# A four-sequence language block: products with Wm, rank rows and the place matrix put ahead of and into the selected attention

## The chip, the cores and the metric

The kernel runs on one core of one Trainium2 chip. The metric is the device time of one execution in microseconds (us), taken as the median of several runs.

## The reference, cut to what matters

The whole is two transformer-like layers over 4 sequences of 1024 tokens with 192 features. The change touches the second half of the first layer (`_L0_ffn_ref`), which routes tokens: 154 of 1024 tokens with the lowest scores get attention, all others a cheap mix.

```python
normed = _ln(hidden_states, g1, b1)
scores = sigmoid(einsum('bld,d->bl', normed, Wr) + br)
_, idx = top_k(-scores, k)            # k = 154
attn_mask = zeros((b, l), bool).at[arange(b)[:, None], idx].set(True)
...                                   # attention of 12 heads over all keys
attn_out = ctx @ Wo + bo
w = scores / (sum(scores, axis=1, keepdims=True) + 1e-06)
pooled = einsum('bl,bld->bd', w, normed)
mix_out = (normed + scores[..., None] * pooled[:, None, :]) @ Wm + bm
merged = where(attn_mask[..., None], attn_out, mix_out)
h = hidden_states + merged
n2 = _ln(h, g2, b2)
ffn = gelu(n2 @ W1 + bf1) @ W2 + bf2
return h + ffn
```

`hidden_states` is itself a layer norm of the stream h, so the kernel needs that norm again for the residual.

## The kernel before, in words

Sequences go in two pairs (loop `p`), and within a pair each sequence has a slot, 0 (`a`) and 1 (`z`). Each engine has its own program, written by hand, and they meet through counting semaphores; nothing is reordered. A sequence is 8 token tiles of 128 tokens (`T = 8`). `XT` holds the normed tokens feature-major (two halves of 96 features and a row of ones for the bias), `X` the normed tokens token-major, `U` the layer's branch to add to `HS`, the stream.

PSUM has eight banks of 512 float32. The four of `ST` are a ring (`ring4`, two for each slot as `o.R2`). Each slot also has two banks `o.D2`: `PV` or `MT`, and `S`.

The order around the change, by TensorE:

- `logits` and `scores_row`: the scores; they are turned into a row (`srow`) and give the pooled sum.
- VectorE `rank_tokens`: compares the score row with each tile's scores; this yields the rank of each token, `notsel` (rank is 154 or more), and `PSEL`, the matrix which gathers the selected tokens. `pool_tokens` follows.
- `pick`: gathers the selected tokens with `PSEL` (L621). ScalarE writes `NTS`.
- `queries0`: queries of the selected tokens in the ring banks (L554), then `values` of all tokens in `o.D2` (L569). ScalarE and VectorE cut the queries into three bfloat16 parts, and SP stores and reloads them in another layout.
- `mix_in` (VectorE, L1440): adds score times pooled vector to `XT`, once `values` has read it.
- `selected`: 6 groups of 4 heads. VectorE reduces ten banks of scores to maxima a group (L1471), alternately in the two `S` banks; TensorE makes the scores (L649, L652), the exponents' arguments (L672) and the sums over values (L685). TensorE's loop `g` issues the maxima of group g+1; those of group 0 come ahead of the loops. Keys of group g+2 are reloaded by DMA once the exponents of group g are through.
- `context` turns the result and, behind it, the ranks (L749). `attended` multiplies with Wo (L757), giving `ATS`.
- `pick_rows` (VectorE): the place matrix `PT` from the turned ranks in PSUM, 8 instructions for the two slots (L1485), and `U` as the norm of `HS` (L1488).
- `mix` and `merge`: for each token tile, the product with Wm (L770) and the placing product `PT` by `ATS` (L772) in the two halves of one bank; VectorE adds the first times `notsel` (L1495), then the second (L1496). Statistics, norm and `turn_norm` follow (L1359, L1369, L536), then the feed-forward (`up`, `back`).

Each call of a float32 matmul appears as two products in the trace, so a token tile's product with Wm is four.

## Time and profile before

| | |
|---|---|
| median of 3 runs | 2040.24 us (2032.58 to 2041.11) |
| the profiled execution | 2034.34 us, of which the span is 2032.3 us |
| TensorE busy | 1658.6 us, 82% of the span |
| VectorE busy | 1377.1 us, 68% |
| ScalarE busy | 955.2 us, 47% |
| GpSimd busy | 126.8 us, 6% |

Busy shares are means over stages with different limits. The granted clock is that of TensorE: 1.00 is 2.4 GHz and 0.50 is 1.2 GHz. Durations of neighbours on one engine overlap by up to 0.2 us, so the time between two starts is the rate.

### The profile page before, as it was taken

What the parts mean: (1) busy time and instruction counts of PE and PEld (TensorE: products, weight loads), DVE (VectorE), ACT (ScalarE), POOL (GpSimd) and SP (SyncE); (2) the same over time, 40 slices, a digit from 0 to 9 for tenths busy, and PEclk for the clock granted to TensorE, in tenths of its full rate; (3) what the DMA queues carried; (4) which work ended last, traced back from release to release, by engine and by line L of the source; (5) the groups of instructions that cost most, each with busy time, mean ns of one, the idle gap of its engine ahead of it and who ended that gap; (6) DMA issues with size and microseconds to landing.
All of it is one profiled execution on the core that took longest, in us unless ns stands there. A gap on an engine that the chain in (4) does not pass through costs nothing.

```text
span 2032.3 us, 26452 instructions
## 1 busy us (share of the span) xinstructions
PE 1658.6 (82%) x9798; PEld 940.1 (46%) x9798; DVE 1377.1 (68%) x3124; ACT 955.2 (47%) x1347; POOL 126.8 (6%) x165
## 2 busy tenths in 40 slices
PE   1676888998999999964456968889899999999444
PEld 1355657564343333363243655766533333336423
DVE  4758565026898989677768576531489989894876
ACT  0421450214777777732532315221357777775153
POOL 5010000000000000005020000000000000000200
PEclk9966895999999999986568778779989999999756
DMA  6003210007001000001010312000431010000001
GB/s 145 1 1 109 76 33 0 0 1 217 24 25 32 24 29 28 1 1 31 0 32 0 109 45 63 1 0 0 125 101 32 24 32 25 24 16 1 0 0 32
DMA packets 53894, 73.39 MB, mean 36 GB/s; under 512 B 18712, under 2 KB 27205, under 8 KB 53767
## 3 DMA queue, kind: packets, MB, share of 16 engines
q1 hardware_dynamic: 52150, 68.54, 11.6%
q0 software_dynamic: 1616, 3.16, 0.7%
q8 instruction: 79, 1.29, 0.3%
q14 instruction: 49, 0.39, 0.1%
HBM read 38.51 MB, written 33.17 MB: 35 GB/s over the span
## 4 chain that ended last, share of the span: by engine, by line
PE 65%; DVE 26%; ACT 3%; issue 3%; DMA 1%; SPq 1%; POOL 0%; DVEq 0%; ACTq 0%
PE PV L888 9%; PE ST L872 8%; PE S L838 6%; PE ST L784 4%; PE ST L554 4%; PE MT L838 3%; PE PV L897 2%; DVE Er L1557 2%; DVE st L1359 2%; PE S L795 2%; DVE nmp L1471 2%; DVE R L1577 2%; DVE amax L1578 2%; PE ST L581 1%; PE S L833 1%
## 5 line engine op out<-in xcount | busy, mean ns | idle before, releaser
L1194 ACT ACTIVATE Er<-ST 128x1024 f32<-128x1024 f32 x384 | 377.0, 1021 | 105.9 <-PE ST L872 105.7
L1533 DVE TENSOR_REDUCE nmp<-S 128x1 f32<-128x512 f32 x514 | 337.2, 682 | 30.8 <-PE S L838 30.8
L872 PE MATMUL ST<-QS,KS 100*128 100x512 bf16 x768 | 218.1, 386 | 0.3
L888 PE MATMUL PV<-Er,V 128*17 128x512 f32 x1536 | 211.8, 601 | 0.0
L838 PE MATMUL S<-KS,QS 96*128 96x512 bf16 x514 | 183.5, 392 | 0.8
L1533 DVE TENSOR_REDUCE nmp<-MT 128x1 f32<-128x512 f32 x254 | 173.2, 682 | 13.5 <-PE MT L838 13.5
L838 PEld LDWEIGHTS S<-KS,QS 96*128 96x128 bf16 x514 | 48.3, 98 | 154.8 <-DVE nmp L1533 118.1
L448 POOL TENSOR_SCALAR tp<-mv 128x8 f32<-128x8 f32 x20 | 5.2, 258 | 1735.7 <-DVE mv L1363 1735.7
L872 PEld LDWEIGHTS ST<-QS,KS 100*128 100x128 bf16 x768 | 72.1, 99 | 64.3 <-ACT Er L1194 5.7
L838 PE MATMUL MT<-KS,QS 96*128 96x512 bf16 x254 | 99.5, 392 | 0.8 <-DVE nmp L1533 0.8
L1471 DVE TENSOR_REDUCE nmp<-S 128x1 f32<-128x512 f32 x120 | 76.5, 684 | 30.7 <-PE S L649 28.6
L784 PE MATMUL ST<-XT,wf 96*128 96x512 f32 x192 | 84.0, 594 | 0.0
L996 PE MATMUL S<-identb,Er 128*128 128x128 bf16 x192 | 24.9, 304 | 72.2 <-DVE Er L1593 72.2
L1161 ACT ACTIVATE Er<-ST 128x480 f32<-128x480 f32 x144 | 64.6, 540 | 31.7 <-PE ST L672 31.5
L1388 DVE TENSOR_TENSOR acc_out<-ST,R 96x512 f32<-96x512 f32 x48 | 32.8, 684 | 67.7 <-ACT R L1115 56.6
L1105 ACT ACTIVATE XT<-PV,cols 96x512 f32<-96x512 f32 x8 | 6.2, 774 | 150.9 <-PE PV L536 150.9
L1212 ACT ACTIVATE R<-ST 128x512 f32<-128x512 f32 x48 | 28.7, 597 | 93.5 <-PE ST L784 93.5
L1501 DVE TENSOR_TENSOR HS<-PV,HS 128x384 f32<-128x384 f32 x8 | 4.5, 557 | 92.5 <-PE PV L796 82.7
L1294 ACT ACTIVATE Er<-S 128x768 bf16<-128x768 bf16 x32 | 25.5, 810 | 80.5 <-PE S L996 80.5
L1196 ACT ACTIVATE Er<-ST 100x1024 f32<-100x1024 f32 x48 | 49.1, 1023 | 28.3 <-PE ST L876 28.3
L888 PEld LDWEIGHTS PV<-Er,V 128*17 128x17 f32 x1536 | 32.4, 96 | 62.2 <-issue 60.5
L1177 ACT ACTIVATE acc_out<-PV 128x512 f32<-128x512 f32 x96 | 57.4, 597 | 7.0 <-PE PV L888 7.0
(392 smaller groups left out, 3285.1 us busy)
## 6 DMA issues: line engine op xcount, KB each, us to landing
KS<-scr_k SPq DMA_DIRECT2D x72, 192.0 KB, 2.6
scr_k<-R SPq DMA_DIRECT2D x16, 576.0 KB, 4.0
QS<-scr_q SPq DMA_DIRECT2D x48, 192.0 KB, 2.8
scr_k<-R SPq DMA_DIRECT2D x16, 384.0 KB, 4.6
QS<-scr_k SPq DMA_DIRECT2D x24, 192.0 KB, 2.6
scr_q<-R SPq DMA_DIRECT2D x8, 576.0 KB, 4.5
scr_k<-R SPq DMA_DIRECT2D x16, 192.0 KB, 5.2
scr_q<-R SPq DMA_DIRECT2D x8, 384.0 KB, 4.9
```

Of the source, the lines that this page charges most:

```text
L554: ins = nc.tensor.matmul(o.R2[i % 2][0:CH, 0:width], w[0:r, c, off + m * CH:off + (m + 1) * CH], src[0:r, c, j * width:(j + 1) * width], s ...
L784: ins = nc.tensor.matmul(o.R2[i % 2], wf1[0:r, c, f * P:(f + 1) * P], o.XT[0:r, c, half * HALF:(half + 1) * HALF], start=c == 0, stop=c == 1)
L795: nc.tensor.matmul(d, o.hid[:, f, t % HT * P:(t % HT + 1) * P], wf2[:, f, :], start=f == 0, stop=False)
L838: ins = nc.tensor.matmul(bank, QS[0:KP, k, (u // 2) * P:(u // 2 + 1) * P], KS[0:KP, k, (u % 2) * HALF:(u % 2 + 1) * HALF], start=True, sto ...
L872: ins = nc.tensor.matmul(ST[i % 2][:, (kt % 2) * HALF:(kt % 2 + 1) * HALF], KS[0:KP + 4, k, kt * P:(kt + 1) * P], QS[0:KP + 4, k, half * H ...
L888: ins = nc.tensor.matmul(PV[row:row + VC, :], slots[h // H].V[:, kt, h % H, :], E[:, step % RING, (kt % 2) * HALF:(kt % 2 + 1) * HALF], st ...
L1161: A_(E0[:, h % RING0, i * 6 * QP:i * 6 * QP + w], ring4[n % 4][:, 0:w], ACT.Exp, scale=float(DH) ** -0.5).then_inc(s["ex0"], 1)
L1177: A_(acc_out[:, part, :], PV[:, :], ACT.Copy).then_inc(s["accout"], 1)
L1194: A_(E[:, g, :], ST[i % 2][:, :], ACT.Exp).then_inc(s["exps"], 1)
L1196: A_(E[0:MS, g, :], ST[i % 2][0:MS, :], ACT.Exp).then_inc(s["exps"], 1)
L1471: v.tensor_reduce(nmp[:, x // 2, x % 2:x % 2 + 1], S[n % 2][:, :], AX.X, ALU.max).then_inc(s["reduced0"], 1)
L1533: v.tensor_reduce(nmp[:, u // 2, u % 2:u % 2 + 1], bank, AX.X, ALU.max).then_inc(s["reduced"], 1)
```

## The change

Seven edits go together.

1. `values` for both slots runs ahead of `pick`, in the ring banks; `queries0` of a slot follows that slot's `pick`.
2. `mix_in` runs ahead of the cut of the queries, and computes `back`, the ratio of the two norms' scales.
3. The products with Wm (`premix`) come after the queries of slot 1. ScalarE evicts them times `notsel` into `U` (`precopy`).
4. The ranks are turned into the ring banks (`turn_rank`), and ScalarE copies them to SBUF (`rank_row`).
5. In `selected`, VectorE puts one instruction (`aside`) behind every second reduction of groups 0 to 3: 16 additions of `X` times `back` into `U`, and 4 rows of the place matrix, now one instruction of 1024 columns from SBUF each.
6. `context` no longer turns the ranks, and `pick_rows` is gone.
7. `mix` has the placing products alone, two tiles a bank, and `merge` adds a bank's two tiles in one instruction.

```diff
@@ -185,6 +185,7 @@
             o.spl = R[0:CH, 0:3 * L].bitcast(BF16).rearrange("p (a c n) -> p a c n", a=3, c=2)
             o.srow = R[:, 3 * L:4 * L]
             o.PT = R[:, 0:2 * L].rearrange("p (q n) -> p q n", q=2)
+            o.rrow = R[:, 2 * L:3 * L]
             o.hid = R[:, 0:FC * HALF].rearrange("p (f n) -> p f n", f=FC)
             o.kc = R[0:CH, 0:3 * HALF].bitcast(BF16).rearrange("p (a n) -> p a n", a=3)
             o.qc = R[0:CH, 3 * HALF:6 * HALF].bitcast(BF16).rearrange("p (a n) -> p a n", a=3)
@@ -217,6 +218,7 @@
             o.cnt = sb("cnt" + nx, [P, 3, T])
             o.rank = sb("rank" + nx, [P, T])
             o.notsel = sb("notsel" + nx, [P, T])
+            o.back = sb("back" + nx, [P, T])
             o.pool3 = sb("pool3" + nx, [CH, 8])
             o.amax = sb("amax" + nx, [P, T])
             o.qsc = sb("qsc" + nx, [P, T])
@@ -560,13 +562,16 @@
 
             def values(p, o, use, w, off):
 
+                banks = (o.R2, o.D2)[use]
+                if use == 0:
+                    pe.wait_ge(s["srow_copied"], at(p, o, 1, 1))
                 for i in range(4):
                     if i >= 2:
                         pe.wait_ge(o.s["vcopied"], p * 8 + 4 * use + i - 1)
                     for t in (2 * i, 2 * i + 1):
                         for c in range(2):
                             r = CH + c
-                            ins = nc.tensor.matmul(o.D2[i % 2][:, (t % 2) * D:(t % 2 + 1) * D], o.XT[0:r, c, t * P:(t + 1) * P],
+                            ins = nc.tensor.matmul(banks[i % 2][:, (t % 2) * D:(t % 2 + 1) * D], o.XT[0:r, c, t * P:(t + 1) * P],
                                                    w[0:r, c, off:off + D], start=c == 0, stop=c == 1)
                     ins.then_inc(o.s["vproj"], 1)
 
@@ -624,10 +629,27 @@
 
             def queries0(p, o):
                 pe.wait_ge(s["nts"], at(p, o, 2, 2))
-                pe.wait_ge(s["srow_copied"], at(p, o, 1, 1))
+                pe.wait_ge(o.s["vcopied"], p * 8 + 4)
                 project(p, o, 4, wq, 0, o.NTS, 2 * QP, 1)
-                values(p, o, 0, wv, 0)
-
+
+            def premix(p, o):
+
+                pe.wait_ge(s["mixin"], at(p, o, 2, 2))
+                for i in range(4):
+                    if i >= 2:
+                        pe.wait_ge(s["precopied"], at(p, o, 4, i - 1))
+                    for t in (2 * i, 2 * i + 1):
+                        for c in range(2):
+                            r = CH + c
+                            ins = nc.tensor.matmul(o.D2[i % 2][:, (t % 2) * D:(t % 2 + 1) * D], o.XT[0:r, c, t * P:(t + 1) * P], wm[0:r, c, :], start=c == 0, stop=c == 1)
+                    ins.then_inc(s["premixed"], 1)
+
+            def turn_rank(p, o):
+
+                pe.wait_ge(o.s["resid"], p * 14 + 6)
+                for t in range(T):
+                    ins = nc.tensor.transpose(o.ST[:, t * P:(t + 1) * P], o.rank[:, t:t + 1].to_broadcast([P, P]), ident[:])
+                ins.then_inc(s["rank_turned"], 1)
 
             def selected(p):
                 base = p * ROWS
@@ -705,10 +727,11 @@
                             turn_sums(a, SUMS0_AT[x])
 
                 for q in slots:
-                    pe.wait_ge(q.s["vcopied"], p * 8 + 4)
-                    pe.wait_ge(q.s["resid"], p * 14 + 6)
+                    pe.wait_ge(s["precopied"], at(p, q, 4, 4))
                 maxima0(0, 0, MAXIMA0)
                 maxrow0(0)
+                for q in slots:
+                    pe.wait_ge(s["rank_copied"], at(p, q, 1, 1))
                 pe.wait_ge(s["qones"], p + 1)
                 for g in range(GROUPS):
                     n = 3 * GROUP * g
@@ -745,9 +768,6 @@
                     for q in range(2):
                         ins = nc.tensor.transpose(o.R2[0][0:CH, (2 * c + q) * QP:(2 * c + q + 1) * QP], o.CX[:, q, c * CH:(c + 1) * CH], ident[0:QP, 0:QP])
                 ins.then_inc(s["ctxt"], 1)
-                for t in range(T):
-                    ins = nc.tensor.transpose(o.D2[t // HT][:, t % HT * P:(t % HT + 1) * P], o.rank[:, t:t + 1].to_broadcast([P, P]), ident[:])
-                ins.then_inc(s["rank_turned"], 1)
 
             def attended(p, o):
                 pe.wait_ge(s["ctxtc"], at(p, o, 1, 1))
@@ -758,18 +778,15 @@
                 ins.then_inc(s["att"], 1)
 
             def mix(p, o):
-                pe.wait_ge(s["mixin"], at(p, o, 2, 2))
+
                 pe.wait_ge(s["pt"], at(p, o, 1, 1))
                 pe.wait_ge(s["atts"], at(p, o, 1, 1))
-                for t in range(T):
-                    if t >= 2:
-                        pe.wait_ge(s["merged"], at(p, o, 8, t - 1))
-                    d = o.D2[t % 2]
-                    for c in range(2):
-                        r = CH + c
-                        nc.tensor.matmul(d[:, 0:D], o.XT[0:r, c, t * P:(t + 1) * P], wm[0:r, c, :], start=c == 0, stop=c == 1)
-                    for q in range(2):
-                        ins = nc.tensor.matmul(d[:, D:2 * D], o.PT[0:QC, q, t * P:(t + 1) * P], o.ATS[0:QC, q, :], start=q == 0, stop=q == 1)
+                for i in range(4):
+                    if i >= 2:
+                        pe.wait_ge(s["merged"], at(p, o, 4, i - 1))
+                    for t in (2 * i, 2 * i + 1):
+                        for q in range(2):
+                            ins = nc.tensor.matmul(o.D2[i % 2][:, (t % 2) * D:(t % 2 + 1) * D], o.PT[0:QC, q, t * P:(t + 1) * P], o.ATS[0:QC, q, :], start=q == 0, stop=q == 1)
                     ins.then_inc(s["mixed"], 1)
 
             def up(p, o, half):
@@ -1019,9 +1036,14 @@
                 for o in slots:
                     scores_row(p, o)
                 for o in slots:
+                    values(p, o, 0, wv, 0)
+                for o in slots:
                     pick(p, o)
-                for o in slots:
                     queries0(p, o)
+                for o in slots:
+                    premix(p, o)
+                for o in slots:
+                    turn_rank(p, o)
                 selected(p)
                 for o in slots:
                     context(p, o)
@@ -1117,10 +1139,26 @@
                         mid(i - 1)
                 mid(group + len(pieces) - 1)
 
+            def precopy(p, o):
+
+                act.wait_ge(s["picks"], at(p, o, 2, 2))
+                for i in range(4):
+                    act.wait_ge(s["premixed"], at(p, o, 4, i + 1))
+                    for t in (2 * i, 2 * i + 1):
+                        ins = A_(o.U[:, t, :], o.D2[i % 2][:, (t % 2) * D:(t % 2 + 1) * D], ACT.Copy, scale=o.notsel[:, t:t + 1])
+                    ins.then_inc(s["precopied"], 1)
+
+            def rank_row(p, o):
+                for n in ("kw0", "kw1"):
+                    act.wait_ge(o.s[n], p * 96 + 48)
+                act.wait_ge(s["rank_turned"], at(p, o, 1, 1))
+                A_(o.rrow[0:QC, :], o.ST[0:QC, :], ACT.Copy).then_inc(s["rank_copied"], 1)
+
             def vcopy(p, o, use):
+                banks = (o.R2, o.D2)[use]
                 for i in range(4):
                     act.wait_ge(o.s["vproj"], p * 8 + 4 * use + i + 1)
-                    A_(o.V[:, 2 * i:2 * i + 2, :, 0:DH], o.D2[i % 2][:, 0:2 * D].rearrange("p (t h d) -> p t h d", t=2, h=H), ACT.Copy).then_inc(o.s["vcopied"], 1)
+                    A_(o.V[:, 2 * i:2 * i + 2, :, 0:DH], banks[i % 2][:, 0:2 * D].rearrange("p (t h d) -> p t h d", t=2, h=H), ACT.Copy).then_inc(o.s["vcopied"], 1)
 
             def inproj(p, o, c):
                 for i in range(4):
@@ -1238,12 +1276,17 @@
                     act.wait_ge(s["srow_turned"], at(p, o, 1, 1))
                     A_(o.srow, o.ST[:, :], ACT.Copy).then_inc(s["srow_copied"], 1)
                 for o in slots:
+                    vcopy(p, o, 0)
+                for o in slots:
                     act.wait_ge(s["gathersel"], at(p, o, 1, 1))
                     for c in range(2):
                         A_(o.NTS[0:CH, c, :], o.S[0:CH, c * 2 * QP:(c + 1) * 2 * QP], ACT.Identity, scale=cols[:, c, 2:3], bias=cols[:, c, 3:4]).then_inc(s["nts"], 1)
                 for o in slots:
                     cut(p, o, 4, pieces_q0(o), 2 * QP)
-                    vcopy(p, o, 0)
+                for o in slots:
+                    precopy(p, o)
+                for o in slots:
+                    rank_row(p, o)
                 selected(p)
                 for o in slots:
                     act.wait_ge(s["ctxt"], at(p, o, 1, 1))
@@ -1436,6 +1479,8 @@
 
             def mix_in(p, o):
                 ve.wait_ge(o.s["vproj"], p * 8 + 4)
+                link(v.reciprocal(o.back[:], o.rnn[:]))
+                v.tensor_tensor(o.back[:], o.back[:], o.rn[:], ALU.mult)
                 for c in range(2):
                     v.scalar_tensor_tensor(out=o.XT[0:CH, c, :], in0=o.srow[0:CH, :], scalar=o.pool3[:, 5 + c:6 + c], in1=o.XT[0:CH, c, :],
                                            op0=ALU.mult, op1=ALU.add).then_inc(s["mixin"], 1)
@@ -1464,6 +1509,19 @@
                         ins = v.tensor_tensor(dst, o.sum0[:, 2 * n:2 * n + 2, 0:DH], o.rec0[:, 2 * n:2 * n + 2].unsqueeze(2).to_broadcast([QP, 2, DH]), ALU.mult)
                     ins.then_inc(s["ctxn"], 1)
 
+                def aside(o, n):
+
+                    if n < T:
+                        if n == 0:
+                            ve.wait_ge(s["precopied"], at(p, o, 4, 4))
+                        v.scalar_tensor_tensor(out=o.U[:, n, :], in0=o.X[:, n, :], scalar=o.back[:, n:n + 1], in1=o.U[:, n, :], op0=ALU.mult, op1=ALU.add)
+                        return
+                    if n == T:
+                        ve.wait_ge(s["rank_copied"], at(p, o, 1, 1))
+                    ins = v.tensor_scalar(o.PT[0:QC, n - T, :], o.rrow[0:QC, :], rowslot[0:QC, n - T:n - T + 1], None, ALU.is_equal)
+                    if n == T + 1:
+                        ins.then_inc(s["pt"], 1)
+
                 for g in range(GROUPS):
                     for x in range(MAXIMA0):
                         n = MAXIMA0 * g + x
@@ -1471,6 +1529,8 @@
                         v.tensor_reduce(nmp[:, x // 2, x % 2:x % 2 + 1], S[n % 2][:, :], AX.X, ALU.max).then_inc(s["reduced0"], 1)
                         if g == GROUPS - 1 and x in SUMS0_AT:
                             divide(a, SUMS0_AT[x])
+                        if x % 2 == 1 and g < 4:
+                            aside(slots[g // 2], g % 2 * 5 + x // 2)
                     ve.wait_ge(s["reduced0"], p * MAXIMA0 * GROUPS + MAXIMA0 * g + MAXIMA0 + 2)
                     if g >= 2:
                         ve.wait_ge(s["mturned"], base + g - 1)
@@ -1478,23 +1538,11 @@
                 for r in range(3):
                     divide(z, r)
 
-            def pick_rows(p, o):
-                ve.wait_ge(s["rank_turned"], at(p, o, 1, 1))
-                for q in range(2):
-                    for j in range(2):
-                        ins = v.tensor_scalar(o.PT[0:QC, q, j * HALF:(j + 1) * HALF], o.D2[j][0:QC, :], rowslot[0:QC, q:q + 1], None, ALU.is_equal)
-                ins.then_inc(s["pt"], 1)
-                for t in range(T):
-                    ins = v.tensor_scalar(o.U[:, t, :], o.HS[:, t, :], o.mv[:, t, 0:1], o.rn[:, t:t + 1], ALU.subtract, ALU.mult)
-                link(ins)
-
             def merge(p, o):
-                for t in range(T):
-                    ve.wait_ge(s["mixed"], at(p, o, 8, t + 1))
-                    d = o.D2[t % 2]
-                    link(v.scalar_tensor_tensor(out=o.U[:, t, :], in0=d[:, 0:D], scalar=o.notsel[:, t:t + 1], in1=o.U[:, t, :], op0=ALU.mult, op1=ALU.add))
-                    v.tensor_tensor(o.U[:, t, :], o.U[:, t, :], d[:, D:2 * D], ALU.add).then_inc(s["merged"], 1)
-                ve.wait_ge(s["merged"], at(p, o, 8, 8))
+                for i in range(4):
+                    ve.wait_ge(s["mixed"], at(p, o, 4, i + 1))
+                    v.tensor_tensor(o.U[:, 2 * i:2 * i + 2, :], o.D2[i % 2][:, 0:2 * D].rearrange("p (t d) -> p t d", t=2), o.U[:, 2 * i:2 * i + 2, :], ALU.add).then_inc(s["merged"], 1)
+                ve.wait_ge(s["merged"], at(p, o, 4, 4))
                 stats(p, o, o.U)
 
             def add(o, i, done):
@@ -1629,11 +1677,10 @@
                     rank_tokens(p, o)
                     pool_tokens(p, o)
                 for o in slots:
+                    mix_in(p, o)
+                for o in slots:
                     cut(p, o, 4, pieces_q0(o), 2 * QP)
-                    mix_in(p, o)
                 selected(p)
-                for o in slots:
-                    pick_rows(p, o)
                 for o in slots:
                     merge(p, o)
                 for o in slots:
```

## Rows read from the trace of the kernel before

**Rows 1.** The page: shares of the chain that ended last, by engine.

```profile
PE 65%; DVE 26%; ACT 3%; issue 3%; DMA 1%; SPq 1%; POOL 0%; DVEq 0%; ACTq 0%
```

**Rows 2.** Windows of the tail: each engine's busy time, granted clock, DMA share, GB/s.

```profile
293.40:349.50 56.10, 45.42 (x180) 44.16 (x180) 32.14 (x113) 1.84 (x4) 2.91 (x4) 0.63 0.00 1
...
1283.00:1339.00 56.00, 45.37 (x180) 44.12 (x180) 32.09 (x113) 1.84 (x4) 2.86 (x4) 0.63 0.00 1
...
308.40:349.50 41.10, 36.19 (x112) 35.68 (x112) 18.09 (x69) 0.00 (x0) 2.91 (x4) 0.50 0.00 1
```

**Rows 3.** Timeline of TensorE in the tail: start, duration, instruction, idle before it.

```profile
297.51 0.48 PE L746 MATMUL ST<-ident,small 80*96 80x80 f32 x4 [1.49 <-DVE small L1464]
...
298.71 2.78 PE L757 MATMUL ST<-wo,NTS 96*80 96x192 f32 x16
...
308.38 1.65 PE L770 MATMUL PV<-wm,XT 96*128 96x192 f32 x4 [4.29 <-DVE U L1496]
...
343.10 1.49 PE L772 MATMUL S<-ATS,R 77*128 77x192 f32 x4
349.51 1.09 PE L536 MATMUL PV<-ident,X 128*96 128x128 f32 x4 [4.92 <-DVE X L1369]
```

**Rows 4.** Timeline of VectorE in the tail.

```profile
296.96 0.49 DVE L1464 TENSOR_TENSOR small<-X 80x32 f32<-80x32 f32 x4
...
321.59 0.42 DVE L1495 SCALAR_TENSOR_TENSOR U<-PV,notsel,U 128x192 f32<-128x192 f32 x1 [1.75 <-PE PV L772]
...
345.47 2.18 DVE L1359 BATCH_NORM_STATS2 st<-U 128x6 f32<-128x192 f32 x8
```

**Rows 5.** Timeline of TensorE ahead of the selected attention.

```profile
175.80 2.70 PE L614 MATMUL MT<-sc,ones 128*96 128x1 f32 x16
...
201.62 6.51 PE L621 MATMUL S<-Er,X 128*96 128x160 f32 x32 [10.63 <-DVE Er L1424]
207.96 1.26 PE L554 MATMUL ST<-NTS,wq 96*96 96x160 f32 x8
209.06 1.47 PE L569 MATMUL PV<-wv,XT 96*128 96x192 f32 x8
```

**Rows 6.** Timeline of VectorE there: end of pooling, cut, first maxima.

```profile
202.30 0.47 DVE L1435 SCALAR_TENSOR_TENSOR pool<-cols,pool 96x1 f32<-96x1 f32 x2
209.41 0.55 DVE L1388 TENSOR_TENSOR acc_out<-ST,small 96x160 f32<-96x160 f32 x2 [6.64 <-ACT small L1115]
...
221.14 2.48 DVE L1440 SCALAR_TENSOR_TENSOR XT<-R,pool,XT 96x1024 f32<-96x1024 f32 x2 [2.99 <-PE S L569]
223.54 6.67 DVE L1471 TENSOR_REDUCE nmp<-S 128x1 f32<-128x512 f32 x10
```

**Rows 7.** Windows of the output projection, which begins at 105.57 after 11.4 us idle.

```profile
105.50:108.30 2.80, 2.73 (x9) 2.73 (x10) 2.76 (x3) 0.00 (x0) 0.00 (x0) 0.50 0.00 0
...
111.60:114.30 2.70, 2.70 (x16) 2.70 (x17) 0.97 (x2) 0.00 (x0) 0.00 (x0) 1.00 0.00 0
```

**Rows 8.** Timeline of ScalarE: one copy of the values.

```profile
219.83 0.49 ACT L1123 ACTIVATE V<-MT 128x384 f32<-128x384 f32 x1 [1.15 <-PE MT L569]
```

**Rows 9.** Timeline of VectorE elsewhere: two instructions like new ones.

```profile
89.93 0.75 DVE L1406 TENSOR_SCALAR R<-R,cols 96x1024 f32<-96x1024 f32 x1
...
382.95 0.56 DVE L1501 TENSOR_TENSOR HS<-PV,HS 128x384 f32<-128x384 f32 x1 [26.56 <-PE PV L796]
```

**Rows 10.** Windows of the loops, the transposes and the feed-forward.

```profile
231.00:243.70 12.70, 12.17 (x90) 7.16 (x88) 7.15 (x13) 6.68 (x15) 0.00 (x0) 0.52 0.21 62
243.70:253.70 10.00, 8.01 (x117) 5.06 (x118) 6.80 (x13) 7.07 (x17) 0.00 (x0) 1.00 0.27 80
...
349.50:356.90 7.40, 6.92 (x32) 5.14 (x33) 6.85 (x14) 5.17 (x7) 0.97 (x1) 0.58 0.00 0
356.90:440.00 83.10, 83.10 (x320) 53.23 (x318) 6.72 (x24) 16.59 (x27) 1.90 (x2) 1.00 0.00 0
```

**Rows 11.** Timeline of TensorE: the first products of a new group's keys.

```profile
253.72 0.59 PE L649 MATMUL S<-QS 96*128 96x512 bf16 x2 [1.29 <-DMA QS<-scr_k]
```

More of the change, by code:

```diff
@@ L248, in build @@
         w2 = slots[0].R[0:CH, 0:2 * F].rearrange("p (t f) -> p t f", t=2)
-        names = """qones loaded consts tokens outproj h1 logit expz score srow_turned srow_copied picks rank_turned pt gathersel nts
+        names = """qones loaded consts tokens outproj h1 logit expz score srow_turned srow_copied picks rank_turned rank_copied premixed precopied pt gathersel nts
             units0 reduced0 units reduced rowmax mturned mcopied acc0 ctxr accout st0 ex0 pv0 ctxn ctxt ctxtc att atts
@@ L1021, in _ @@
                 for o in slots:
+                    values(p, o, 0, wv, 0)
+                for o in slots:
                     pick(p, o)
+                    queries0(p, o)
                 for o in slots:
-                    queries0(p, o)
+                    premix(p, o)
+                for o in slots:
+                    turn_rank(p, o)
                 selected(p)
```

## The prediction

> **What bounds the kernel now.** I read the page first, and in it the chain that ended last: it is 65% TensorE and 26% VectorE [rows 1]. No engine bounds the whole, so the change has to be read in the stages it touches. There are two pairs of sequences, and every engine works through a pair in the same order, so each stage counts twice; the windows have the tail stage of pair 1 at 56.1 us and 0.63 of the clock, and pair 2's at 56.0 and 0.63 [rows 2]. All other numbers below are of pair 1.
>
> The tail stage runs from the last turned sums of the selected attention (293.4) to the first transpose of the third norm (349.5). TensorE's timeline [rows 3] and VectorE's [rows 4] show what sets it. VectorE ends the last division at 297.4. TensorE still turns the ranks, then does `attended` (298.71 to 301.32), fills slot 0's two banks and waits 4.29 us until VectorE has made the place rows and U. From 308.38 to 344.4 it then runs 28 groups of four products back to back, and VectorE waits 1.75 us for each later token tile [rows 4]. In this stretch the granted clock is 0.50, the 1.2 GHz level [rows 2]: four products take 1.28 us (36.0/28), against 0.65 in the values' projection of the same width (1.47 for eight, of which 0.16 overlaps the next) [rows 3, 5]. So 16 of the 32 groups (the Wm half) and all the preparation on VectorE sit on the path. After them come statistics, X and the transposes: 345.47 to 349.51, 4.0 us [rows 3, 4].
>
> Ahead of the selected attention the chain is the ranking on VectorE, pick of slot 1 (201.62 to 208.1), slot 0's queries and values, slot 1's queries and values, and last the mixing of XT, which lets the first maximum start at 223.54 [rows 5, 6]. Before that pick TensorE is idle for 10.63 us (from 191.0), and the pooling ends at 178.5 [rows 5]; slot 0's pick lies between, as long as slot 1's.
>
> **The change, part by part.**
>
> *Values ahead of the picks, in the ring banks.* The values are 8 groups of 1.3 us. They begin at 178.5, after the pooling; the wait for the copied score row costs nothing, as that copy ran during the pooling. The clock is low there. The output projection, of the same width, also starts low, after 11.4 us idle: its first products are at 0.50, and from 6 us on, with waits between, 16 take 2.70 us at 1.00 [rows 7], so I take it that the clock rises after some 4 us. Taking that: 10.5 + 2 = 12.5 us, to 191. Slot 0's pick follows, then idle until slot 1's ranks at 201.6. Nothing is late. If the clock never rose, values would take 21 us (to 199.3), slot 0's pick 6.6 more, and slot 1's pick would start at 206 to 208 instead of 201.6: up to 6.4 us lost. If the shorter idle time kept the clock high in slot 1's pick, its 6.5 us could shrink to some 4.3: 2.2 won. I take zero, the pick as it was, since 4 us of idle are left in front of it and after as long an idle (the 4.29 us before 308.38) TensorE came back low [rows 3].
>
> *Mixing of XT before the query cut.* VectorE is free from 202.8 to 209.4 [rows 6]. Four mixing instructions of 1.24 and two small ones per slot make 5.8 us, to 208.6. It fits ahead of the cut at 209.4, which is set by ScalarE. Were it not to fit, every us over goes to the queries' reload.
>
> *Queries of slot 1, products with Wm, ranks turned.* After pick (208.1) ScalarE copies 0.9, queries take 1.1 [rows 5]: 210.2. Products with Wm: 8 groups x 1.31 = 10.5: 220.7. Their eviction by ScalarE, 16 copies of 192 columns, is bounded by half of the 384-column one's 0.49 and by the whole [rows 8], 0.5 to 1.0 a group, under TensorE's 1.31: hidden; without that cover it would be 8 us at most. Turning the ranks is two times eight columns of 128, by width 128/192 of 1.31, 0.9: 222.5. That also covers the new wait of the first maxima for the last of these copies. The first maximum follows 0.4 later, 222.9, where it was 223.54 as VectorE was still mixing XT: 0.6 won. The rank rows' copies (two of 1024 columns, some 1 us each from 0.49 for 384) wait also for the keys' stores, long issued; behind them is the maxima row's copy, needed only when the maxima of group 0 are reduced, so they are hidden. SP's queue gets slot 1's query store some 6 us sooner, and no DMA is added.
>
> *Twenty insertions on VectorE in the maxima of groups 0 to 3.* Sixteen additions into U have 192 columns; the nearest row is 0.42 from PSUM [rows 4], of which neighbours overlap some 0.08: 0.34 each. Four place rows of 1024 in SBUF: 0.75 [rows 9]. Group 0 runs alone, VectorE without a gap (223.54, ten in 6.67 [rows 6]), so 5 x 0.34 = 1.7 us go on the path. Group 1 is reduced while TensorE runs its first loop at the low clock, 12.7 us for VectorE's 7.15 [rows 10]: hidden. Groups 2 and 3 lie in loops of 10 us with 6.8 us of VectorE work [rows 10]. There the chain is: last exponent products of the loop, reload of the keys, next products at 253.72, 1.29 us late [rows 11]. Two insertions ahead of the second half move its last reductions by some 0.7 (two of 0.34), so 0.7 each loop. The two place rows of group 3 stand behind the reduction that TensorE waits for and (1.5) fall into the reload's wait, which itself moves by the 0.7. Sum: 1.7 + 0.7 + 0.7 = 3.1 lost. Bounds: 0 if all is hidden, 16 x 0.42 + 4 x 0.75 = 9.7 if nothing is.
>
> *The tail.* Removed: 16 rank transposes behind the context, eight place rows from PSUM and the sixteen of U, 64 products with Wm, and one of two VectorE steps a tile. Now: division ends 297.4, context 0.4, `attended` 2.6: 300.5. The first placing group is 0.65, its addition of 384 columns 0.56 [rows 9]. Two banks alternate at about 0.75 a group: slot 0's fourth addition ends at 304.0. Statistics 2.9: 306.9. Slot 1's first two groups wait ready; two additions 1.1 to 308.0; its other two groups start at 307.6 after 3 us of idle, taken at the low clock (1.28 each), last addition ended 310.9. Then 4.0 as before: 314.9 against 349.51, so 34.6 won. All placing at the high clock: 36; all at the low one: 31.6.
>
> Here a page speaks. The Trainium skill, TensorE: Matmul & The Clock Gate, What's actually happening, says that the clock is low by default and that activity releases it. The trace does not bear that out here, with 0.50 held over 36 us of busy products [rows 2, 3]. By the rule the placing would soon be fast and the tail's gain nearer 36 than 34.6.
>
> *Sum.* Per pair 34.6 + 0.6 - 3.1 = 32.1, for two 64.2. The profiled execution took 2034.34 us (span 2032.3): 1970.1. The median of the runs shown is 5.9 higher, which would give 1976. I say 1971.
>
> **Rivals.**
>
> *The loops fall to the low clock.* The first loop is at 0.52 with 12.7 us, the others at 1.00 with 10 [rows 10]. Insertions thin TensorE's work; if they keep it low for four more loops, 2.7 x 4 = 10.8 a pair. For it: the first loop stays low although busy. Against: loops 1 and 2 keep their 8.0 us of TensorE work and grow by only 0.7. Time: 2034.3 - 2 x 21.3 = 1992.
>
> *Values at the low clock.* The products of one column ahead of them are no dense work. Against: the output projection, which rose by itself [rows 7]. 6.4 a pair: 1983.
>
> *The low clock has a time of its own.* It held from 308 to 356 whatever ran. If it holds some 45 us after the short placing too, 30 to 35 us of the first feed-forward products run at half rate, 17 a pair lost: 2034.3 - 2 x 15 = 2004. Against: in the row of the transposes alone the clock rises (0.58 over the 7.4 us, 0.50 before, 1.00 after) [rows 2, 10]. The Trainium skill, same page, Part 4: PE-mode transpose, says that transposes do not engage the high clock, which would leave the feed-forward to begin low; by it a few us a pair are added, and the row just named speaks against it.
>
> *Slower than before.* The same low clock held through the whole feed-forward (83.1 us, all at 1.00 [rows 10]): each us of its work costs one more. It decides from 32 us of such work on (64 us at the low clock); in full, 2034.3 + 2 x (83.1 - 32.1) = 2136. For it: the products with Wm never left 0.50 [rows 2]. Against: the feed-forward ran at 1.00 once the transposes had gone before, and they still do.
>
> *No change.* If the removed work were not on the path. The chain holds the 28 groups one after another with no other engine between them, so only a loss elsewhere could hide it.
>
> **How the numbers follow.** Forecast 0.77; values low 0.06; loops low 0.08; clock with its own time 0.05; slower 0.02; nothing 0.02. The forecast's own range takes 36 and 31.6 for the tail, 0 and half of 9.7 for the insertions, and 2.2 won in the pick: 2034.3 - 2 x 38.8 = 1957 would need all at once, so I stop at 1960; the other end, 31.6 - 4.8 + 0.6 = 27.4, is 1980. To leave out no more than 2 in 10 it reaches to the loops' 1992. A measurement of this kernel tells about 0.5% from no change. Faster by over 0.5%: 0.96; within: 0.02; slower: 0.02.
>
> **What would show it.** Tail window 293.4 to the transposes: 56 to about 21.5 us, no product with Wm in it, and VectorE's waits for a tile gone. Values at 178 to 191, the first half at 0.50. First maximum near 222.9. Ten first reductions with five insertions 8.4 us instead of 6.7. Loops 1 and 2 longer by 0.7, loop 0 and the last two as before. Feed-forward at 1.00, 83 us. The prediction is wrong if loops show 0.5 clock, if slot 1's pick starts after 202, or if the feed-forward begins low for more than a few us.

## The result and the profile after

The changed kernel takes 1993.01 us (median of 4 runs, 1979.84 to 1995.26), the kernel before 2040.67 (4 runs, 2032.58 to 2042.37). The ratio is 0.9763, 95% interval 0.9742 to 0.9784. The direction was forecast; the size was not. Between the two profiled executions 64.2 us were forecast and 42.4 came (span 2032.3 to 1989.9); the measured time lies 1 us above the range's end of 1992.

The change did what it says. TensorE's timeline of the changed kernel has the values as one block ahead of the pick, and after the queries the products with Wm and the turned ranks:

```profile
176.97 14.03 PE L574 MATMUL ST<-wv,XT 96*128 96x192 f32 x64
190.83 4.51 PE L626 MATMUL S<-Er,X 128*96 128x160 f32 x32
...
200.27 6.26 PE L626 MATMUL S<-Er,X 128*96 128x160 f32 x32 [2.65 <-DVE Er L1467]
207.48 1.33 PE L556 MATMUL ST<-NTS,wq 96*96 96x160 f32 x8 [0.94 <-ACT NTS L1283]
208.65 1.47 PE L644 MATMUL PV<-wm,XT 96*128 96x192 f32 x8
...
219.10 1.91 PE L651 MATMUL ST<-ident,rank 128*128 128x128 f32 x16
220.85 0.60 PE L671 MATMUL S<-KS,QS 96*128 96x512 bf16 x2
```

These answer to [rows 5]. Up to slot 1's pick all runs 1.35 us earlier than before. The surprise is in the tail, pair 1 first, then pair 2:

```profile
300.12 0.77 PE L769 MATMUL ST<-ident,small 80*96 80x80 f32 x4 [2.37 <-DVE small L1509]
300.69 5.33 PE L777 MATMUL ST<-wo,NTS 96*80 96x192 f32 x16
305.81 2.77 PE L789 MATMUL PV<-ATS,R 77*128 77x192 f32 x8
...
323.73 2.77 PE L789 MATMUL S<-ATS,R 77*128 77x192 f32 x8
331.17 1.09 PE L538 MATMUL PV<-ident,X 128*96 128x128 f32 x4 [4.68 <-DVE X L1412]
...
1271.93 0.48 PE L769 MATMUL ST<-ident,small 80*96 80x80 f32 x4 [2.37 <-DVE small L1509]
1272.24 4.45 PE L777 MATMUL ST<-wo,NTS 96*80 96x192 f32 x16
1276.53 1.46 PE L789 MATMUL PV<-ATS,R 77*128 77x192 f32 x8
...
1285.88 2.58 PE L789 MATMUL MT<-ATS,R 77*128 77x192 f32 x8 [1.38 <-DVE U L1544]
1288.25 2.77 PE L789 MATMUL S<-ATS,R 77*128 77x192 f32 x8
1295.70 1.09 PE L538 MATMUL PV<-ident,X 128*96 128x128 f32 x4 [4.68 <-DVE X L1412]
```

Three things are to be seen against [rows 3]. A bank of two tiles takes eight placing products, not four. The idle time before slot 1's context turn has grown from 1.49 to 2.37 us, as the turned ranks that stood there are gone. And `attended` took 2.78 before and now 5.33 and 4.45: the clock is low from the gap on, in pair 1 for the whole placing (2.56 a bank), while in pair 2 it rises within `attended` (1.30 a bank) and falls again behind a wait of 1.38 us ahead of the last two banks. The windows say it in clocks (columns as in [rows 2]): whole tail of either pair, pair 1's `attended` and its placing, loops 1 and 2 of pair 1, and the feed-forward.

```profile
295.97:331.17 35.20, 28.16 (x100) 26.53 (x100) 14.39 (x65) 1.84 (x4) 2.92 (x4) 0.55 0.00 0
1267.77:1295.70 27.93, 19.50 (x101) 17.74 (x101) 14.30 (x65) 1.84 (x4) 2.93 (x4) 0.77 0.00 1
300.69:305.81 5.12, 5.12 (x19) 4.17 (x18) 0.00 (x0) 0.92 (x2) 0.00 (x0) 0.50 0.00 0
305.81:331.17 25.36, 20.68 (x65) 20.18 (x64) 11.17 (x47) 0.49 (x1) 2.92 (x4) 0.50 0.00 0
...
242.20:252.80 10.60, 8.37 (x117) 5.07 (x117) 8.23 (x18) 6.85 (x17) 0.00 (x0) 1.00 0.25 76
252.80:265.30 12.50, 9.86 (x117) 5.49 (x118) 8.90 (x18) 6.41 (x15) 0.00 (x0) 0.86 0.25 65
...
338.50:422.00 83.50, 83.50 (x322) 53.39 (x320) 6.72 (x24) 16.66 (x27) 1.90 (x2) 1.00 0.00 1
```

Between marks that both kernels have (start of slot 1's pick; first maxima row turned; the sums' turn; first transpose of the norm) the two traces compare so, in us:

| stretch | before, pair 1 / 2 | after, pair 1 / 2 | won | forecast |
|---|---|---|---|---|
| start to pick, pair 1; norm to pick, pair 2 | 201.6 / 842.0 | 200.3 / 842.1 | 1.4 / -0.2 | 0 |
| pick to maxima row | 29.3 / 29.3 | 29.3 / 29.3 | 0 / 0 | -1.1 |
| maxima row to sums' turn (loops) | 62.5 / 62.2 | 66.4 / 65.2 | -4.0 / -3.1 | -1.4 |
| sums' turn to transpose (tail) | 56.1 / 56.1 | 35.2 / 27.9 | 20.9 / 28.2 | 34.6 |
| last transpose mark to the end | 693.2 | 694.2 | -1.0 | 0 |

The column "won" adds up to 42.4 before rounding. Of the 21.8 missing, 20.1 lie in the tails and 4.2 in the loops; the stretch from pick to maxima row gives 2.2 back.

### The profile page after: what moved, and what is told of

Read it like the earlier page. It is cut to its first block, busy times and chain, and to the rows that moved or that the text cites. A ratio compares the mean times of both kernels' runs of the same rounds, so it can differ in the third digit from the quotient of the medians.

```text
span 1989.9 us, 26444 instructions
## 1 busy us (share of the span) xinstructions
PE 1642.2 (83%) x9798; PEld 919.7 (46%) x9798; DVE 1356.8 (68%) x3076; ACT 971.2 (49%) x1383; POOL 126.8 (6%) x165
## 4 chain that ended last, share of the span: by engine, by line
PE 64%; DVE 26%; ACT 4%; issue 3%; DMA 2%; SPq 1%; POOL 0%; DVEq 0%; ACTq 0%
PE PV L905 9%; PE ST L889 8%; PE S L855 6%; PE ST L801 4%; PE ST L556 4%; PE MT L855 3%; PE PV L914 2%; DVE nmp L1529 2%; DVE Er L1605 2%; DVE st L1402 2%; PE S L812 2%; DVE R L1625 2%; DVE amax L1626 2%; PE ST L586 1%; PE S L850 1%
## 5 line engine op out<-in xcount | busy, mean ns | idle before, releaser
L889 PEld LDWEIGHTS ST<-QS,KS 100*128 100x128 bf16 x768 | 72.1, 99 | 64.2 <-ACT Er L1232 5.7
L1013 PE MATMUL S<-identb,Er 128*128 128x128 bf16 x192 | 24.8, 303 | 72.2 <-DVE Er L1641 72.2
L905 PEld LDWEIGHTS PV<-Er,V 128*17 128x17 f32 x1536 | 32.3, 95 | 62.2 <-issue 60.5
L1625 DVE TENSOR_TENSOR R<-R,g2bc 128x768 f32<-128x768 f32 x32 | 30.7, 958 | 43.6 <-ACT acc_out L1258 42.9
```

The costliest lines, as they stand in the source:

```text
L889: ins = nc.tensor.matmul(ST[i % 2][:, (kt % 2) * HALF:(kt % 2 + 1) * HALF], KS[0:KP + 4, k, kt * P:(kt + 1) * P], QS[0:KP + 4, k, half * H ...
L905: ins = nc.tensor.matmul(PV[row:row + VC, :], slots[h // H].V[:, kt, h % H, :], E[:, step % RING, (kt % 2) * HALF:(kt % 2 + 1) * HALF], st ...
L1625: link(v.tensor_tensor(o.HG[:, t % HT, :], o.HG[:, t % HT, :], g2bc[:], ALU.mult))
```

## The experiments

Two theories stood against each other at the start: that the clock was lost in the wait which the removed rank transposes had partly filled, or that placing products lose it by themselves; and for the loops, that the insertions cost the time, or the clock.

**1. The gap filled.** The changed kernel with idle work in the gap:

```diff
                 ins.then_inc(s["ctxt"], 1)
+                if o is a:
+                    for t in range(24):
+                        nc.tensor.transpose(a.D2[t // HT % 2][:, t % HT * P:(t % HT + 1) * P], ident[:], ident[:])
```

> The changed kernel, with 24 transposes of the identity behind the first context turn of each pair, results unused. They fill the 2.37 us in which TensorE waits for the last division. Theory: removing the rank transposes opened that gap, the clock fell in it, and attended and placing of pair 1 ran at 1.2 GHz (5.33 us and 2.56 us a bank) while pair 2 rose again half way (4.45 and 1.30). Then both pairs show attended at 2.6 to 2.9 and placing at 1.30 a bank, the tail from the sums' turn to the first transpose of the norm is 24 to 27 us in both, and the time is 1978 to 1983. Rival: placing products of 77 rows pull the clock down by themselves, or it falls whatever fills the gap: attended fast, placing still 2.56 in pair 1, time 1988 to 1995.

1979.15 us, all four runs between 1979.04 and 1979.74; ratio to before 0.972 (0.9697 to 0.9743). Timeline of pair 1, then windows of pair 1's gap, `attended` and placing, and pair 2's placing:

```profile
302.35 0.60 PE L773 MATMUL S<-ident 128*128 128x128 f32 x4
302.79 0.44 PE L769 MATMUL ST<-ident,small 80*96 80x80 f32 x4
303.07 2.78 PE L780 MATMUL ST<-wo,NTS 96*80 96x192 f32 x16
305.68 1.46 PE L792 MATMUL PV<-ATS,R 77*128 77x192 f32 x8
...
315.03 1.57 PE L792 MATMUL MT<-ATS,R 77*128 77x192 f32 x8 [1.39 <-DVE U L1547]
316.44 1.46 PE L792 MATMUL S<-ATS,R 77*128 77x192 f32 x8
```

```profile
298.54:303.07 4.53, 4.53 (x45) 4.53 (x46) 3.22 (x18) 0.43 (x1) 0.00 (x0) 1.00 0.00 0
303.07:305.68 2.61, 2.61 (x19) 2.39 (x17) 0.00 (x0) 0.92 (x2) 0.00 (x0) 1.00 0.00 0
305.68:322.57 16.89, 10.83 (x66) 10.24 (x64) 11.07 (x47) 0.49 (x1) 2.92 (x4) 0.97 0.00 1
...
1265.56:1282.94 17.38, 11.32 (x66) 10.52 (x64) 11.06 (x47) 0.49 (x1) 2.92 (x4) 0.83 0.00 0
```

More work on TensorE, and 14 us less in all, as expected (1978 to 1983). The tails are 24.0 and 24.5 us instead of 35.2 and 27.9. The first six banks run at the high clock in both pairs; in pair 2 the clock falls once more within the last bank (1.95 us), behind a wait of 1.38 us. The gap is the cause of the clock lost ahead of the placing: in all six profiled tails that have it unfilled (this case's changed kernel, experiments 5 and 10) `attended` has a granted clock of 0.50 to 0.70, and in all ten with the gap filled (experiments 1 and 6 to 9) it takes 2.6 us at 1.00.

**2. One removal undone.** The changed kernel with the 16 rank transposes back in `context`, for both slots, their results unused (in the diff they are the lines that the change takes out).

> The changed kernel with one removal undone: the 16 transposes of the ranks stand behind the context turns again, their results unused. Theory: they covered part of the wait for the last division (1.49 us left of 2.37), so that the clock was not lost there. Then attended takes 2.6 us and a placed bank 1.30 in both pairs, as in the gap-filled kernel, and the time is 1978 to 1984. Rival: 1.49 us idle is as good as 2.37 for the fall: attended at 4 to 5 us in at least one pair, 1985 to 1995.

1980.76 us (1978.81 to 1983.91), ratio 0.9723 (0.9707 to 0.974), as expected. `attended` runs at 1.00 again in both pairs, with the idle time ahead of slot 1's context turn back at 1.5 us:

```profile
300.67 0.48 PE L769 MATMUL ST<-ident,small 80*96 80x80 f32 x4 [1.50 <-DVE small L1511]
...
313.83 2.75 PE L791 MATMUL MT<-ATS,R 77*128 77x192 f32 x8 [1.38 <-DVE U L1546]
```

```profile
296.52:301.87 5.35, 3.85 (x37) 3.62 (x38) 3.22 (x18) 0.87 (x2) 0.00 (x0) 1.00 0.00 0
301.87:304.48 2.61, 2.61 (x18) 2.39 (x17) 0.00 (x0) 0.49 (x1) 0.00 (x0) 1.00 0.00 0
304.48:323.81 19.33, 13.27 (x66) 12.47 (x64) 11.07 (x47) 0.49 (x1) 2.92 (x4) 0.75 0.00 1
```

So this one removal, which the prediction booked as a gain, cost some 12 us as it was made. One part of the expectation failed: not all banks take 1.30. Slot 1's last two, behind the wait of 1.38 us shown above, run at the low clock (2.75 us). This wait stands in ten profiled tails that reach it at the high clock, and in nine of them the clock falls before the placing ends; experiment 8 takes the wait away.

**3. The same cure in the kernel before.** 40 transposes in slot 0's `mix`, ahead of the third tile, in the 4.29 us of [rows 3]:

```diff
                 for t in range(T):
+                    if o is a and t == 2:
+                        for u in range(40):
+                            nc.tensor.transpose(a.R2[0][:, u % HT * P:(u % HT + 1) * P], ident[:], ident[:])
                     if t >= 2:
```

> The kernel before, with 40 transposes of the identity in slot 0's mix ahead of its third token tile, in the 4.29 us in which TensorE waits for VectorE. Results unused. Theory: that idle time is what dropped the clock to 1.2 GHz, and the products with Wm and the placing kept it there for 36 us. Filled, 28 groups take 0.65 to 0.8 us instead of 1.28, VectorE's two steps of 0.77 a tile bound the stretch, and it shrinks by 13 to 16 us a pair: 2034 - 2 x 15 gives 2004 to 2014. Rival: the products themselves lower the clock within a few us: 2030 to 2040, as before.

2021.6 us (2018.78 to 2024.87), ratio 0.9923 (0.9897 to 0.9949): a gain, but under what was expected. The windows show the stretch at the high clock as long as it is fed, and slot 1's last six tiles at the low one. Between them TensorE waits 1.87 us for slot 1's bank, while VectorE makes slot 0's statistics.

```profile
321.98 1.21 PE L773 MATMUL MT<-wm,XT 96*128 96x192 f32 x4 [1.87 <-DVE U L1499]
```

```profile
302.99:320.00 17.01, 17.01 (x117) 16.65 (x116) 13.18 (x37) 0.03 (x1) 0.00 (x0) 1.00 0.00 1
322.00:337.00 15.00, 15.00 (x48) 14.76 (x48) 4.46 (x12) 0.00 (x0) 1.31 (x1) 0.52 0.00 0
```

The expectation was wrong by leaving out that second wait. The theory holds up to that wait: from the high clock, 17 us of products with Wm, placing and filler stay there while fed. In the kernel before, about 8 us a pair of the tail were a matter of the clock, not of work.

**4. The values ahead, alone.** The kernel before with the first edit only (`values` before `pick` in the ring banks, queries behind each pick).

> The kernel before, with only the first edit: values of both slots ahead of the picks in the ring banks, queries of a slot behind its pick. Theory: it brings the queries of slot 1 and the start of the selected attention forward. After the pick of slot 1 TensorE has 1.1 us of queries left instead of 13.1, but the reload of slot 0's queries lands only some 5 to 6 us after the cut at 210.7 and VectorE still has the mixing of XT: first maximum near 217 to 219 instead of 223.5, so 4 to 6 us a pair, 2022 to 2030. Rival: the keys and queries reload sets the start: 0 to 2 us a pair, 2030 to 2038.

2028.65 us (10 runs), ratio 0.9955 (0.9938 to 0.9972), within the 2022 to 2030 expected. Slot 1's pick to the first maxima row takes 24.7 and 24.8 us instead of 29.3, and the timeline shows why not less:

```profile
211.35 1.33 PE L554 MATMUL ST<-NTS,wq 96*96 96x160 f32 x8 [0.94 <-ACT NTS L1249]
220.64 1.01 PE L651 MATMUL S<-KS,QS 96*128 96x512 bf16 x2 [7.95 <-DMA QS<-scr_q]
```

TensorE then waits 7.95 us for the reload of the queries. In the changed kernel the products with Wm and the turned ranks end at 220.85, 20.6 us after slot 1's pick began; here the reload lands 16.5 us after it. Most of the Wm work thus replaces a wait, and some 4 us of it do not.

**5. The insertions moved.** Slot 0's eight additions go behind the first eight reductions of group 1, all others behind the last group's maxima row, where VectorE is idle for 9.9 us:

```diff
-                        if x % 2 == 1 and g < 4:
-                            aside(slots[g // 2], g % 2 * 5 + x // 2)
+                        if g == 1 and x < T:
+                            aside(a, x)
...
+                for n in range(T, T + 2):
+                    aside(a, n)
+                for n in range(T):
+                    ins = aside(z, n)
+                link(ins)
+                for n in range(T, T + 2):
+                    aside(z, n)
                 for r in range(3):
                     divide(z, r)
```

> The changed kernel, with the same 20 insertions at other places: the eight additions of slot 0 behind the first eight reductions of group 1 (the loop at the low clock), all others in the 9.9 us in which VectorE is idle after the last group. Theory: the insertions cost 4.9 us in pair 1 and some 3.5 in pair 2, most of it in loop 2 (12.4 and 11.8 us instead of 9.8), by a late maxima row and a short fall of the clock. Then loops 1 to 3 are back at 9.8 to 10 us, group 0 takes 6.7, and the time falls by 8 us to 1983 to 1987. Rival: the loops' fall of the clock comes from the new order ahead of them, and stays: loop 2 over 11 us, at most 3 us won.

1996.33 us (1992.55 to 1998.44): 9 us above the range expected, and no gain. From first product to maxima row group 0 takes 7.33 us instead of 8.68, but loops 1 to 4 take 48.5 and 47.2 us together instead of 45.0 and 43.9: the clock falls in more of them, in pair 1 also in loops 3 and 4, which never had an insertion. Windows of group 0 and loops 1 to 4, pair 1:

```profile
219.90:227.23 7.33, 3.91 (x18) 0.88 (x16) 6.68 (x13) 1.34 (x2) 0.00 (x0) 0.87 0.60 158
239.22:248.36 9.14, 8.02 (x126) 5.08 (x117) 6.79 (x13) 5.99 (x14) 0.00 (x0) 1.00 0.25 69
248.36:260.09 11.73, 9.57 (x121) 5.51 (x117) 6.91 (x13) 6.56 (x15) 0.00 (x0) 0.85 0.25 69
260.09:273.53 13.44, 10.88 (x121) 6.40 (x118) 7.18 (x13) 6.45 (x15) 0.00 (x0) 0.75 0.20 58
273.53:287.72 14.19, 11.06 (x138) 7.33 (x131) 10.23 (x32) 6.55 (x15) 0.00 (x0) 0.88 0.06 16
```

So the clock falls without insertions too. A loop may lose it for a few us, and which one does differs from kernel to kernel. Nor do the loops explain the whole: in this profile the tail of pair 2 ran at the low clock throughout (35.0 us, 27.9 in the changed kernel), so that a gain from the new places can't be read from the total. Experiments 6 and 7 have the gap filled. That theory of mine fell, and the next run takes up what is left of it.

**6. The loops' waits filled too.** The gap-filled kernel, and 12 transposes at the head of the maxima of groups 2 to 4, into a part of the `MT` bank that nothing reads then:

```diff
                 def maxima0(g, x0, x1):
+                    if x0 == 0 and 2 <= g <= 4:
+                        for t in range(12):
+                            nc.tensor.transpose(MTf[0:CH, 384:512], ident[:, 0:CH], ident[:])
```

> The gap-filled kernel (first experiment) and besides 12 transposes of the identity, results unused, behind the maxima row of loops 1 to 3, where TensorE waits 0.6 to 2 us for the next keys. Theory: in the loops TensorE is busy for 8.0 of some 10 us and its clock falls now and then, about once a pair, which costs 2 us each; filled waits keep it at 1.00 in loops 1 to 3. Then no window of these loops is under 0.95, at most 0.4 us a loop is added where the filler outlasts the wait, and the time is 1974 to 1979. Rival: the falls come in the products themselves, not in the waits: loops as before with 1.3 us of filler added, 1980 to 1988.

1986.67 us (1982.72 to 1994.52): 7.5 us more than in the first experiment by the medians (the intervals of the ratios just overlap), and a miss against the 1974 to 1979 expected. The clock did what was expected in the filled loops, 0.99 or 1.00 in all six; the next loop, unfilled, fell to 0.89 in pair 2 and took 14.9 us. And the filler outlasts the waits: loop 1 takes 11.1 and 11.0 us instead of 9.9 and 10.1 in the first experiment, and loop 3, which has no insertion, 10.0 in both pairs instead of 9.1 and 8.8.

**7. Moved and filled.**

> As the kernel with loops filled, and the 20 insertions moved as in the second experiment (slot 0's additions in group 1, all others after the last group). Theory: the insertions cost 1.1 to 1.3 us in group 0 and 0.9 in each of loops 1 and 2, which the second experiment hid behind more falls of the clock (five against one). With the waits filled, first maxima to first maxima row takes 7.5 us instead of 8.7, loops 1 to 3 take 9.7 to 10.1, and the time is 3 us a pair under the kernel with loops filled: 1968 to 1973. Rival: moving them is what makes the clock fall: loops at 0.75 to 0.88 again, 1980 or more.

The "second experiment" of this text is number 5 here.

1975.97 us (1975.48 to 1978.43), ratio 0.9704 (0.9688 to 0.972). 11 us under the run before by the medians, 7.4 by the profiled spans: group 0 at 7.6, and the loops of pair 1 at full clock:

```profile
221.71:229.29 7.58, 4.37 (x18) 0.90 (x16) 6.79 (x13) 1.34 (x2) 0.00 (x0) 0.76 0.52 145
239.94:249.88 9.94, 9.30 (x129) 6.38 (x129) 6.80 (x13) 5.99 (x14) 0.00 (x0) 1.00 0.25 75
...
259.87:269.89 10.02, 9.38 (x133) 6.32 (x130) 6.79 (x13) 6.28 (x15) 0.00 (x0) 1.00 0.27 80
```

The expectation was 1968 to 1973; filled loops of pair 2 took 10.4 to 10.7. Against the gap-filled kernel (1979.15) it is 3 us less, and the intervals of the two ratios overlap.

**8. And slot 1's first additions ahead of slot 0's statistics.**

```diff
-                for o in slots:
-                    merge(p, o)
+                merge(p, a, range(4))
+                merge(p, z, range(2))
+                ve.wait_ge(s["merged"], at(p, a, 4, 4))
+                stats(p, a, a.U)
+                merge(p, z, range(2, 4))
+                ve.wait_ge(s["merged"], at(p, z, 4, 4))
+                stats(p, z, z.U)
```

> As the kernel moved and filled, and besides slot 0's statistics stand behind slot 1's first two additions. Theory: slot 0's statistics hold back slot 1's additions, and TensorE waits 1.4 us for a free bank; with the order changed that wait goes, the last placing product ends 1.3 us sooner, but one addition more is late: 0.8 to 1.3 us a pair, 1966 to 1972. Rival: the four additions left behind the statistics take it back: no difference to the kernel moved and filled.

1974.33 us (1969.05 to 1976.22), ratio 0.9683 (0.9665 to 0.9701). First placing product to first transpose:

```profile
304.56:320.87 16.31, 10.56 (x66) 10.27 (x65) 10.98 (x47) 0.49 (x1) 2.93 (x4) 0.93 0.00 1
1262.40:1278.70 16.30, 10.56 (x65) 10.27 (x64) 10.97 (x47) 0.49 (x1) 2.92 (x4) 0.86 0.01 2
```

Against 18.7 and 17.4 in the kernel moved and filled: the wait of 1.4 us for a bank is gone from both, and with it the fall of the clock behind it: all eight banks take 1.30 in both pairs. In whole time it misses the 1966 to 1972 expected, and its interval overlaps the one above. It has the lowest median of the kernels that compute the whole, some 19 us under the changed one.

**9. Half the placing.** The gap-filled kernel with four products a bank; the rows of ranks 77 to 153 are left out.

> The gap-filled kernel, with only the first half of each placement (the ranks 0 to 76; the other half of the selected tokens' rows is left out): 4 products a bank instead of 8. Theory: the prediction counted 4 products a bank where there are 8, and this is the greater part of the clock-free error in its tail. Then a bank takes 0.65 us, and from the first placing product to the first transpose it is 13.0 to 14.5 us, as the prediction's sum had it (14.4), where the gap-filled kernel has 16.9 and 17.4. Rival: VectorE's additions and statistics set this stretch, and the count does not matter: 16 to 17.4 us.

1970.2 us. The stretch is 14.6 and 13.9 us, where 16.9 and 17.4 were with eight products:

```profile
302.11:316.73 14.62, 7.26 (x34) 6.13 (x33) 11.07 (x47) 0.49 (x1) 2.92 (x4) 0.70 0.00 0
1259.27:1273.16 13.89, 6.53 (x33) 5.41 (x33) 11.07 (x47) 0.49 (x1) 2.92 (x4) 0.78 0.01 2
```

The prediction's sum had 14.4, also with the last two banks at the low clock. With the count that it used, it comes out.

**10. The changed kernel again.**

> The changed kernel once more, unchanged, to see how often it lies near 1980 and how often near 1993. Theory: the clock is lost in the 2.37 us gap in one pair or in both, as the gap happens to lie, and each loss costs some 10 to 12 us; so the times are in two or three groups, near 1980, 1992 and perhaps 2000, while the gap-filled kernel had all four within 0.7 us. Rival: the spread comes from the loops alone: times spread evenly over a few us.

1994.76, 1992.72, 1987.25, 1992.77, 1982.38. Its profiled execution shows the same as the first: pair 1's `attended` at 0.50 and 25.4 us from placing to transpose, pair 2's at 0.60 and 19.2. The times do not fall into clean groups as the theory had it, so something besides the tails moves them; the loops are likely. The run at 1979.84 has a mean granted clock of 0.883, the other three of its set 0.878; that it had the high clock in both tails is not shown, as it was not profiled.

## Why the prediction was wrong, point by point

*The tail, forecast at 21.5 us, took 35.2 and 27.9.* Two steps failed.

- "division ends 297.4, context 0.4, `attended` 2.6". `attended` took 5.1 and 4.3 us, and pair 1's placing 2.56 a bank. The step took the clock for high there, having looked at idle time only ahead of slot 1's placing. The rank transposes were booked as work removed at no cost; the idle time between them was not. Experiments 1 and 2 show it: the tails are 24.0 and 24.5 with the gap filled, so the clock is worth 11.2 and 3.4 us. The smaller wait ahead of slot 1's last two banks the prediction had right: it took them at the low clock.
- "The first placing group is 0.65". That is a single tile's price, and a bank holds two tiles now: 1.30. With eight banks this makes 10.4 us of products instead of 5.2, of which 2.3 and 3.5 come to bear (experiment 9). It was a miscount and no matter of hardware.

What the prediction said of the bounds of the tail ("all at the low one: 31.6") was thus wrong as well: it had half the products and left `attended` out. By the prediction's own steps, slot 0's four groups at 1.28 instead of 0.75 add 2.1 us, so 34.6 becomes 32.5 and not 31.6. Had the count and `attended` been right, it would have held the measured time.

*The loops, forecast at 1.4 lost, lost 4.0 and 3.1.* Loop 1 went from 9.95 to 10.63 between first products, as said. But pair 1 of the gap-filled kernel has the insertions and no fall of the clock in loops 1 to 4, and these take 43.4 us where they took 41.1 before: 2.3 lost without a fall, where 1.4 were forecast. One fall in loop 2 of either pair (0.86, 12.5 us) is the rest; with it pair 1 of the changed kernel takes 45.0. The rival named it, but as a state of four loops at 2.7 us each, caused by the insertions; it came once a pair at 1.6 us here, and experiment 5 shows that it comes without them. That this rival's 1992 lies 1 us from the measured time is a coincidence: most of the loss is in the tails.

*Group 0 and the front: right in sum, not in terms.* 0.6 won and 1.7 lost were forecast; measured is 0. From the start of slot 1's pick the first maximum came 0.9 us sooner, and the ten reductions with five insertions took 7.6 us instead of 6.7, 0.9 more and not 1.7. An insertion costs what was said (0.33 from start to start). But without any the ten take 6.23 in experiment 5 and took 6.67 before, where TensorE's clock fell within them (0.73 over the stretch) and its products set part of the pace; the new order runs them at VectorE's own pace. Of the four us of idle time forecast ahead of slot 1's pick, 2.65 stand there and 0.94 ahead of slot 0's queries, which now lie between the picks; slot 0's pick ran at the high clock (4.51 instead of 6.57). Slot 1's pick began low behind the 2.65 us and took 6.26, as forecast.

*Values first.* Nearly right: the first 4.0 us at 0.50, but the next 9.8 at 0.86, so the rise came later than the 4 us taken; the block took 13.9 us and not 12.5, and nothing was late by it.

*The low clock with a time of its own, and slower than before.* Neither: the feed-forward runs at 1.00 over 83.5 us. Ahead of it the transposes of the norm began at the low clock and ended at the high one, as in [rows 10]. The page that the prediction weighed (the Trainium skill, TensorE: Matmul & The Clock Gate) says in its section What's actually happening that activity releases the clock. Pair 1's tail, 0.50 over 25.4 us with TensorE busy for 20.7 of them, again does not bear that out. The section HAM oscillation — how this bites in real kernels, of the same page of the Trainium skill, says that waits between bursts of matmuls throttle it; experiments 1 and 2 agree in kind, but the waits of its example are given as about 3 to 5 us, and here 2.37 us were enough.

*What stays open.* Why busy placing products do not bring the clock back, while `attended` did in pair 2, was not tried. Nor is it settled what picks the loop that loses the clock, or why a wait of one length costs it at one place and not at another: in the changed kernel's pair 1 TensorE waits 2.00 us for the keys of loop 4 and runs on at 1.00.

```profile
276.01 0.59 PE L671 MATMUL S<-QS 96*128 96x512 bf16 x2 [2.00 <-DMA QS<-scr_k]
```

```profile
276.00:286.70 10.70, 8.96 (x124) 5.98 (x124) 9.81 (x31) 5.45 (x12) 0.00 (x0) 1.00 0.01 2
```

## What to carry to other kernels

Before work is removed or moved from a wait of TensorE, ask what the wait becomes: 1.75 us a pair of useless transposes, half of them in the gap, were worth 12 us here in all. Idle work can be worth more than a better order, but only as far as it fits a true wait; beyond that it costs its own time (experiment 6). And count the products of a fused group from the loop, tiles times halves, before a price from another loop is put on it.

## What the runs showed of the hardware

- TensorE's clock went to 0.50 in or shortly behind a wait of 2.37 us in all six profiled tails that have it, and in none of the eight with 1.49 us at the same place (the kernel before, experiments 2 to 4). In the kernel before with its gap filled it was low behind a wait of 1.87 us, and nine of ten waits of 1.38 us between placing products were followed by the low clock before the placing ended. But a wait of 2.00 us in a loop left it at 1.00: the length alone does not tell.
- Once low, it stayed so through 20.7 us of products within 25.4 us (pair 1 of the changed kernel). The same products ran at 1.00 over all eight banks in experiment 8, which began them at it and had no wait among them.
- The changed kernel's times spread over 15 us (1979.84 to 1995.26); with the one gap filled, over 0.7 us in four runs. With the loops filled as well they spread over 12 us again (1982.72 to 1994.52), so the gap is not the only source.
